# Attention probabilities weighed in blocks of two groups, eight blocks per image instead of fourteen, with a third buffer of probabilities

## What is computed

```
qkv  = (groupnorm(xn) @ w_proj.T + b_proj)      # 4 heads, 16 channels per head, 784 tokens
attn = softmax(q k^T * 16**0.5, axis=2)         # per head 784 x 784
h    = attn v  ->  h @ w_out.T + b_out;  h = h * sigmoid(h) + xs
```

## Time and profile before

| | us |
|---|---|
| median of 3 runs (1763.51 to 1764.68) | 1763.89 |
| time of the profiled execution | 1766.6 |
| its span, first to last instruction | 1763.9 |
| TensorE matmul busy | 1597.4 (91%) |
| VectorE busy | 1292.2 (73%) |
| ScalarE busy | 1023.8 (58%) |
| GpSimd busy | 455.2 (26%) |

### The profile page before, as it was taken

How to read it: one execution, slowest core, us unless ns; L and a number is a source line. 1 busy time by engine, 2 the same in 40 slices (tenths; PEclk the granted TensorE clock), 3 DMA queues, 4 the chain that set the end, 5 groups by cost and what they waited for, 6 DMA issues and landing times.

```text
span 1763.9 us, 30283 instructions
## 1 busy us (share of the span) xinstructions
PE 1597.4 (91%) x10848; PEld 730.4 (41%) x10848; DVE 1292.2 (73%) x2666; ACT 1023.8 (58%) x1401; POOL 455.2 (26%) x364
## 2 busy tenths in 40 slices
PE   0699869999686799999999999999999999999997
PEld 0333335555575234444344444444444444444332
DVE  5677557887787687787677777877778778777762
ACT  0000156676132157777677777777777777777676
POOL 0400011110300313234233242333333423333212
PEclk9999989999897689999999999999999999999999
DMA  8122166665000423322333234323332343233300
GB/s 204 32 53 52 31 96 108 108 100 92 1 0 1 64 33 50 50 43 35 52 50 50 44 41 63 49 34 50 51 52 44 40 63 50 34 52 50 52 12 19
DMA packets 71213, 92.82 MB, mean 53 GB/s; under 512 B 23516, under 2 KB 64340, under 8 KB 70960
## 3 DMA queue, kind: packets, MB, share of 16 engines
q1 hardware_dynamic: 67728, 89.59, 31.3%
q0 software_dynamic: 3360, 1.61, 1.3%
HBM read 9.00 MB, written 6.42 MB: 9 GB/s over the span
## 4 chain that ended last, share of the span: by engine, by line
PE 76%; DVE 10%; DMA 5%; ACT 3%; SPq 3%; issue 2%; POOL 1%; DVEq 0%; ACTq 0%
PE ps L1050 19%; PE ps L1040 16%; PE ps L985 14%; PE ps L860 8%; PE ps L884 5%; DVE arena L1430 3%; PE ps L899 3%; DMA arena<-arena 3%; PE ps L1006 2%; ACT arena L678 2%; PE ps L946 2%; DMA x<-x_in 2%; SPq L431 2%; PE ps L1023 1%; PE ps L1014 1%
## 5 line engine op out<-in xcount | busy, mean ns | idle before, releaser
L1430 DVE TENSOR_REDUCE arena<-ps 128x1 f32<-128x392 f32 x1600 | 826.4, 561 | 258.5 <-PE ps L985 246.8
L791 ACT ACTIVATE arena<-ps 112x784 f32<-112x784 f32 x896 | 704.2, 822 | 232.2 <-PE ps L1040 224.9
L985 PE MATMUL ps<-arena 112*128 112x392 bf16 x1536 | 483.8, 341 | 16.2 <-DMA arena<-arena 8.2
L1040 PE MATMUL ps<-arena 114*112 114x392 bf16 x1792 | 443.3, 334 | 6.6 <-ACT arena L791 5.9
L1050 PE MATMUL ps<-arena 112*32 112x392 f32 x3584 | 391.2, 508 | 0.5 <-ACT arena L791 0.5
L985 PEld LDWEIGHTS ps<-arena 112*128 112x128 bf16 x1536 | 149.3, 97 | 367.2 <-DVE arena L1430 301.7
L1040 PEld LDWEIGHTS ps<-arena 114*112 114x112 bf16 x1792 | 228.1, 133 | 107.2 <-ACT arena L791 38.8
L884 PE MATMUL ps<-arena 96*128 96x392 f16 x768 | 142.2, 336 | 22.1 <-DMA arena<-arena 16.6
L678 ACT ACTIVATE arena<-ps,magic,arena 128x784 f32<-128x784 f32 x128 | 128.2, 1005 | 37.0 <-PE ps L884 36.8
L860 PE MATMUL ps<-arena 128*64 128x392 f32 (+1 forms) x768 | 139.7, 506 | 3.9 <-DMA arena<-arena 3.9
L1050 PEld LDWEIGHTS ps<-arena 112*32 112x32 f32 x3584 | 70.7, 108 | 141.8 <-issue 140.0
(11 more groups left out here) (142 smaller groups left out, 1383.7 us busy)
## 6 DMA issues: line engine op xcount, KB each, us to landing
arena<-arena SPq DMA_DIRECT2D x504, 73.5 KB, 2.7
arena<-arena SPq DMA_DIRECT2D x256, 84.2 KB, 2.7
x<-x_in SPq DMA_DIRECT2D x8, 784.0 KB, 21.0
out<-x SPq DMA_DIRECT2D x16, 392.0 KB, 2.9
arena<-arena SPq DMA_DIRECT2D x252, 24.5 KB, 2.4
arena<-arena SPq DMA_DIRECT2D x256, 1.5 KB
arena<-arena SPq DMA_DIRECT2D x16, 225.0 KB, 3.4
arena<-arena SPq DMA_DIRECT2D x16, 224.8 KB, 2.9
```

The costliest lines, as they stand in the source:

```text
L791: nc.scalar.activation(probs[w % 2][:, 2 * pair:2 * pair + 2, :], two(2 * place, rows=slice(0, TT)), ACT.Exp).then_inc(s_taken, 1)
L985: last = nc.tensor.matmul(ps[:, bank, 0:CH], q[0:ROWS_L, h, it * 128:(it + 1) * 128], k[0:ROWS_L, h, c * CH:(c + 1) * CH], start=True, sto ...
L1040: last = nc.tensor.matmul(ps[0:TT, 2 * place + j, 0:CH], ks[s % 4][0:ROWS_ALL, h, jt * TT:(jt + 1) * TT], qs[s % 4][0:ROWS_ALL, h, c * CH: ...
L1430: nc.vector.tensor_reduce(mx[img % 2][:, c, v:v + 1], scores, AX.X, ALU.max).then_inc(s_mf, 1)
```

## The change

The table `WEIGHED` takes the place of `weighed(u)`. Groups 0 and 7, the first of each half of queries, are still weighed alone, in units 3 and 17. The others are weighed two at a time, back to back, in units 7, 11, 15, 21 and 25, and the last two in unit 1 of the next image. The earlier group of each pair is thereby weighed two units later than before; the later one stays where it was. `probs` has three buffers in turn over the whole layer in place of two, and the exponential of a group waits for the weighing of the group three earlier in place of two. Nothing is computed differently.

```
-        probs = [part([TT, NH, CH]) for _ in range(2)]
+        probs = [part([TT, NH, CH]) for _ in range(PROBS)]         # PROBS = 3
...
-        def weighed(u):
-            return (u - 3) // 2 if u % 2 else None
+        WEIGHED = {3: [0], 7: [1, 2], 11: [3, 4], 15: [5, 6], 17: [7], 21: [8, 9], 25: [10, 11]}
+        LAST_WEIGHED = [NW - 2, NW - 1]
...
-                        if s >= 1 or w >= 2:
-                            act.wait_ge(s_pv, lin(lambda t: NW * t + w - 1, s, i, 4))
-                        nc.scalar.activation(probs[w % 2][:, 2 * pair:2 * pair + 2, :],
+                        if NW * s + w >= PROBS:
+                            act.wait_ge(s_pv, NW * s + w + 1 - PROBS)
+                        nc.scalar.activation(probs[(NW * s + w) % PROBS][:, 2 * pair:2 * pair + 2, :],
...
-                    w = weighed(u)
-                    if w == -1 and s >= 1:
-                        weigh(s - 1, NW - 1)
-                    elif w is not None and w >= 0:
+                    if u == 1 and s >= 1:
+                        for w in LAST_WEIGHED:
+                            weigh(s - 1, w)
+                    for w in WEIGHED.get(u, []):
                         if w == 0 and s >= 1 or w == NT:
-                            pe.wait_ge(s_acc, lin(lambda t: 2 * t + w // NT, s, i, 4))
+                            pe.wait_ge(s_acc, 2 * s + w // NT)
                         weigh(s, w)
```

More of the change, by code:

```diff
@@ L32 @@
 NM = NH * QT + 1
+PROBS = 3
 DEN_ROWS = 28
@@ L1050, in weigh @@
                     last = nc.tensor.matmul(ps[32 * h:32 * h + 32, BANK_ACC, 0:CH], vs[s % 4][:, jt, h, :],
-                                            probs[w % 2][:, h, :], start=(jt == 0), stop=(jt == NT - 1),
+                                            probs[(NW * s + w) % PROBS][:, h, :], start=(jt == 0), stop=(jt == NT - 1),
                                             tile_position=(0, 32 * h))
@@ L1144, in _ @@
             pe.wait_ge(s_taken, n)
-            weigh(B - 1, NW - 1)
+            for w in LAST_WEIGHED:
+                weigh(B - 1, w)
             pe.wait_ge(s_head, B)
```

## The result

The changed kernel takes 1824.85 us in the median of four runs (1823.20 to 1827.52), the kernel before 1764.29 beside it (1763.51 to 1766.53). The ratio is 1.0343, with a 95% interval of 1.0325 to 1.036. 1826 was forecast. The profiled execution took 1827.52 us, its span is 1825.7.

What follows compares the result with a forecast made beforehand. TensorE was taken to bound the layer, VectorE and ScalarE close behind. Stretches summed to +2.36 us per even and +1.64 per odd image, +64 over 16 pairs, less 2: +62 on 1766.6, median 1826, range 1780 to 1852.

Steps and rivals of the forecast that it cites:

- TensorE bounds, the others are near: Attention layer before the change: TensorE busy 97%, VectorE 75%, ScalarE 73%, so their place in time counts.
- The price of the second group: Second weighing in a block: two more passes on TensorE, 0.67 us in place of 0.90, saving 0.23 per merge.
- The rival that merging saves nothing: Blocks of two: each group keeps its 0.90 us, 45 us more, 1871 us in all; chance 7 in 100.
- VectorE's chain: Plain stretch from block to block: reductions and the wait for a bank make it 4.65 us, +0.17 on 4.48.
- ScalarE's, 4.34: Plain stretch from block to block: ScalarE's exponentials let the next block's chunk 0 start 4.34 us after the last.
- 15 to 17, 1 to 3, 17 to 21, 3 to 7, even 21 to 25: Stretches between weighings in these units, in order: +0.67, +0.67, 0, -0.19 (even) or -0.38 (odd), +0.67 us.
- Odd 21 to 25: Units 21 to 25, odd images: ScalarE's exponentials through units 22 and 23 give 5.07 against 4.93 us, +0.14.
- Even 11 to 15: Units 11 to 15, even images, with the sums' spread at u = 14: left at the plain stretch's +0.17 us.
- the chance that it grows: Spread at u = 14, even images: might wait 0.3 us more for its DMA, adding 5 us to the total.
- The ends: First image without a block in unit 1, last one without chunks: 2 us taken off the sum.
- The third buffer at nothing: Third buffer of probabilities: costs memory, no instruction and no time, as its wait ends long before.

Runs made afterwards that it cites:

- the pairs with short maxima and exponentials: Half the columns of each maximum, then of each exponential too, left out; groups alone against blocks, three buffers: 1745.44 against 1786.28 us, then 1742.30 against 1757.91.
- all short and blocks: Changed kernel with half the columns of maxima, exponentials, ScalarE's take-outs and tanh left out: 1744.83 us, against 1741.46 with the same left out and groups alone.

## Why the prediction was right, point by point

- *TensorE bounds, the others are near.* Right. The step that decided it, that a wall between two chunks and light units behind it give the lead to VectorE, is shown by the pairs with short maxima and exponentials.
- *The price of the second group* (0.67): measured 0.65 to 0.66. A merge saves 0.25, not 0.23, where nothing else binds. The rival that merging saves nothing is excluded by 4.24 from block to block.
- *VectorE's chain, 4.65*: 4.67 to 4.68, with the very four reductions in the chain. *ScalarE's, 4.34*: 4.40.
- *15 to 17, 1 to 3, 17 to 21, 3 to 7, even 21 to 25*: all within 0.06 us.
- *Odd 21 to 25*, +0.14 forecast, +0.35 measured. The sized term left something out: the sums' spread at u = 24 needs a place of the ring as well. ScalarE's and TensorE's rows after the change:

```profile
1069.68 2.28 ACT L792 ACTIVATE arena<-ps 112x784 f32<-112x784 f32 x3 [1.40 <-PE ps L1041]
...
1070.56 0.54 PE L1041 MATMUL ps<-arena 114*112 114x392 bf16 x2 [0.25 <-ACT arena L792]
...
1071.36 0.32 PE L1032 MATMUL ps<-arena 8*128 8x392 f16 x1
...
1072.15 0.54 PE L1041 MATMUL ps<-arena 114*112 114x392 bf16 x2
```

  The second exponential of the row ends at 1069.68 + 0.72 + 0.82 = 1071.22, L1032 starts 0.14 later, and its own 0.79 us come only then. I had let them lie beside the wait. With short maxima and exponentials the blocks make this stretch 0.12 shorter, so it is ScalarE's chain that makes it longer here.
- *Even 11 to 15*, +0.17 forecast, -0.54 measured: the sum's largest error, 0.7 x 14 = 10 us. Half of it is the DMA's wait (0.37), which I left as it was, naming only the chance that it grows. Its cause, the output write started beside it, stood in the queues of before, and I had not read them. The other half (0.34) is the block's own term. I gave it VectorE's chain of a plain stretch, but the spread makes this one 5.45 long for TensorE without any wait, and the block shortens it by 0.17. That the spread gives VectorE the time to keep up is argued, no run takes it apart.
- *The ends*, 2 us taken off, should have been added: they gave some 6 us more than three middle images. The last images have few chunks or none and wait for ScalarE, and in each the granted clock then fell to 0.50 for 3.4 us (from 1774.2 and 1804.9), so that a block took 2.68 and 2.74 us to the next score in place of 1.46, about 1.2 of the 3.8 and 5.1 us. Images 6 and 28 with their fall of the clock before lay on the other side, some 7 us, and I had neither. So 8 us at the ends and about 7 from terms each a little too small (odd 21 to 25 above all) stand against these 7 and the 10 of the point above. It is luck that they nearly cancel: the total of 1826 is closer than its terms.
- *The third buffer at nothing*: right.

## What to carry to other kernels

A switch that costs an engine 0.25 us can be worth more than it costs when it spaces that engine's work: with few buffers to the engines behind it, an even rhythm is what keeps all three busy. Before work is gathered into blocks, work out for one period when the slower consumer gets its first and its last input, and compare that with the producer's own time; here two lines of sums gave 4.65 against 4.25 us, and the chip 4.68. And a unit of work that moves pays in full where it arrives, but gives back only what the next bound leaves where it left.

## What the runs showed of the hardware

A small DMA (two issues, 1.33 us together) took 0.7 to 0.8 us more to come through when a write of 392 KB to DRAM started within 0.6 us of it. It landed 3.86 us after its issue in the median of even images 4 to 28, against 3.17 with the write 17 us ahead and 3.07 after the change; in image 10 the 16 engines were busy 53% of the stretch, against 15% after. TensorE's granted clock fell from 1.00 to 0.50 behind waits of 1.49 us (kernel before, image 6) and 1.16 us (image 10 with all short and blocks), and 3.4 or 6.8 us at that clock cost 1.2 to 2.0 us at 15 to 17 alone. And f32 passes on 32-column parts may follow bf16 ones of the same layout at no cost (0.18 us after them), so the way in and out of 0.24 us belongs to the layout and not to the type.
